# A bank for each row block of the output projection, V transposed later, V's low half behind the scaling of P

## The reference

```python
q = (x @ wq).reshape(B, S, 32, 128)      # k, v: 8 heads; rope on q and k
scores = einsum('bqhgd,bshd->bhgqs', qg, k) * 128 ** -0.5
allowed = (j <= i) & (j > i - 128)       # sliding window
attn = softmax(where(allowed, scores, min), axis=-1)
out = einsum('bhgqs,bshd->bqhgd', attn, v).reshape(B, S, 4096)
x = x + out @ wo
```

## Time and profile before

| | us |
|---|---|
| median of 3 runs (746.28 to 747.5) | 746.47 |
| the profiled execution, its own time | 746.33 |
| its span | 744.6 |
| PE busy | 717.2 |
| DVE busy | 601.0 |
| ACT busy | 413.3 |
| POOL busy | 396.5 |

### The profile page before, as it was taken

How to read it: one execution, slowest core, us unless ns; L and a number is a source line. 1 busy time by engine, 2 the same in 40 slices (tenths; PEclk the granted TensorE clock), 3 DMA queues, 4 the chain that set the end, 5 groups by cost and what they waited for, 6 DMA issues and landing times.

```text
span 744.6 us, 13949 instructions
## 1 busy us (share of the span) xinstructions
PE 717.2 (96%) x3692; PEld 603.1 (81%) x3692; DVE 601.0 (81%) x2060; ACT 413.3 (56%) x1122; POOL 396.5 (53%) x466
## 2 busy tenths in 40 slices
PE   8899789999999999999999999999999999998998
PEld 5787667888888888888888888888888888887786
DVE  6898778877887888878887888788878887788795
ACT  3324475657655676556655766576656665754320
POOL 0674268634864477438653765367535863462420
PEclk9999999999999999999999999999999999999999
DMA  8240003100220022002200120013000310030002
GB/s 266 73 158 16 0 3 98 43 1 2 73 70 1 0 70 70 0 0 70 56 14 0 56 70 14 0 32 94 15 0 0 99 28 1 1 114 1 0 31 85
DMA packets 25843, 32.13 MB, mean 43 GB/s; under 512 B 5833, under 2 KB 14281, under 8 KB 25298
## 3 DMA queue, kind: packets, MB, share of 16 engines
q1 hardware_dynamic: 25232, 30.69, 13.1%
q10 hardware_dynamic: 578, 1.05, 0.4%
HBM read 27.54 MB, written 4.19 MB: 43 GB/s over the span
## 4 chain that ended last, share of the span: by engine, by line
PE 70%; DVE 20%; issue 5%; ACT 3%; DMA 1%; POOL 1%; DVEq 0%; SPq 0%; ACTq 0%
PE bank L1102 26%; PE bank L1160 19%; PE bank L1145 6%; PE bank L1124 5%; PE bank L1068 5%; PE bank L1132 3%; DVE prob L822 2%; DVE rot L787 2%; DVE oT_lo L834 2%; DVE prob L814 1%; DVE sm L807 1%; PE bank L1121 1%; DVE rot L778 1%; ACT prob L550 1%; DVE pT_hi_lo L828 1%
## 5 line engine op out<-in xcount | busy, mean ns | idle before, releaser
L368 POOL TENSOR_TENSOR swap<-swap,rope 128x512 f32<-128x512 f32 x80 | 110.1, 1377 | 129.8 <-ACT swap L523 129.8
L550 ACT ACTIVATE prob<-sm,nmax 128x128 f32<-128x128 f32 x128 | 51.5, 403 | 151.4 <-DVE prob L814 150.4
L375 POOL TENSOR_SCALAR_AFFINE_SELECT pT_hi_lo<-pT_hi_lo 128x256 fp32r<-128x256 f32 x128 | 52.3, 409 | 140.3 <-DVE pT_hi_lo L828 139.8
L523 ACT ACTIVATE swap<-bank 64x512 f32<-64x512 f32 x160 | 94.9, 593 | 10.6 <-PE bank L1102 6.7
L558 ACT ACTIVATE pT_hi_lo<-bank 128x256 fp32r<-128x256 f32 x128 | 48.9, 382 | 71.5 <-PE bank L1132 50.6
L822 DVE TENSOR_SCALAR prob<-prob,rinv 128x128 f32<-128x128 f32 x256 | 83.3, 367 | 4.5
L385 POOL TENSOR_TENSOR q_lo<-rot,q_hi 128x512 fp32r<-128x512 f32 x64 | 82.6, 1291 | 6.9 <-ACT q_hi L531 6.9
L1160 PE MATMUL bank<-wo_hi,oT_hi 128*128 128x512 f32 x256 | 74.6, 413 | 5.0 <-DVE x L841 5.0
L828 DVE TENSOR_TENSOR pT_hi_lo<-bank,pT_hi_lo 128x256 fp32r<-128x256 f32 x128 | 53.6, 418 | 29.4 <-ACT pT_hi_lo L558 29.2
L1102 PE MATMUL bank<-xnT_hi,wq_hi 128*128 128x512 f32 x256 | 71.4, 391 | 2.2 <-DVE v_lo L798 1.4
L1102 PE MATMUL bank<-xnT_lo,wq_hi 128*128 128x512 f32 x256 | 73.4, 389 | 0.0
(11 more groups left out here) (150 smaller groups left out, 1768.9 us busy)
## 6 DMA issues: line engine op xcount, KB each, us to landing
raw<-in_L_attn_wq SPq DMA_DIRECT2D x32, 256.0 KB, 3.0
raw<-in_L_attn_wo SPq DMA_DIRECT2D x32, 256.0 KB, 2.6
x<-in_L_attn_x SPq DMA_DIRECT2D x4, 512.0 KB, 7.3
raw<-in_L_attn_wk SPq DMA_DIRECT2D x8, 256.0 KB, 2.7
raw<-in_L_attn_wv SPq DMA_DIRECT2D x8, 256.0 KB, 2.6
out<-x SPq DMA_DIRECT2D x8, 256.0 KB, 2.0
raw<-in_L_ffn_W_base ACTq DMA_DIRECT2D x4, 256.0 KB, 5.1
wb_keep_hi<-q_hi SPq DMA_DIRECT2D x1, 1024.0 KB, 4.9
```

The lines of the kernel that those rows point to most:

```text
L368: nc.gpsimd.tensor_tensor(w, w, tab, ALU.mult).then_inc(t2_done, 1)
L523: last = nc.scalar.activation(swap[a:a + half, m % 2, :], A[m % 2][b:b + half, :], ACT.Copy)
L550: last = nc.scalar.activation(prob[:, s % 2, lo:hi], src, ACT.Exp, bias=nmax[:, s % 2, i:i + 1], scale=-1.0, accum_out=rsum[:, s % 2, i:i ...
```

## The change

`out_project` of row block 1 writes bank 5 (`O[0]`, whose contents have been read by then) instead of bank 7, except for the very last one. It no longer waits for the add of row block 0. In exchange `values`, which overwrites bank 5, waits for the add of the block before, and row block 0 for the add that last read bank 7. `v_transpose` stands behind the first four matmuls of a half's first slot. On DVE `v_lo` moves behind `softmax_norm` in slot 0, and the add of row block 0 behind it in slots 3 and 7.

```diff
+        def wo_bank(beta, i, last):
+            return C if i == 0 or last else O[0]
...
-                        if s == 0 and not (last and hf == 1):
-                            v_lo(2 * g + hf, hf)
-                        if s % G == 3 and not start:
-                            x_add(beta - 1, (b - 1) % BATCH, 0)
                         if s % G == 0 and not (first and b < 2):
                             x_add(beta - 2, (b - 2) % BATCH, 1)
                         softmax_norm(u, s)
+                        if s == 0 and not (last and hf == 1):
+                            v_lo(2 * g + hf, hf)
+                        if s % G == 3 and not start:
+                            x_add(beta - 1, (b - 1) % BATCH, 0)
...
 # values
                 wait(pe, otlo_done, 2 * beta)
+                wait(pe, x_added, 2 * beta)
...
 # out_project
-                wait(pe, x_added, 2 * beta + i)
+                if i == 0:
+                    wait(pe, x_added, 2 * beta - 1)
+                elif last:
+                    pe.wait_ge(x_added, 2 * beta + 1)
...
-                        last = mm(C[:, :], oT[a][:, par, i, h, :], wo_s[c][:, h, :],
+                        end = mm(wo_bank(beta, i, last)[:, :], oT[a][:, par, i, h, :], wo_s[c][:, h, :],
...
 # group, PE
-                        if s == 0 and not start:
-                            v_transpose(j)
...
-                            project(j + 1, 1 - hf, FIRST[s], FIRST[s + 1], g + hf)
+                            mid = FIRST[s] + 4 if s == 0 and not start else FIRST[s]
+                            project(j + 1, 1 - hf, FIRST[s], mid, g + hf)
+                            if s == 0 and not start:
+                                v_transpose(j)
+                            project(j + 1, 1 - hf, mid, FIRST[s + 1], g + hf)
```

More of the change, by code:

```diff
@@ L835, in o_lo, with x_add @@
                                             oT[0][:, par, i, :, :].bitcast(F32), ALU.subtract).then_inc(otlo_done, 1)
-            def x_add(beta, b, i):
+            def x_add(beta, b, i, last=False):
                 dve.wait_ge(c_done, 2 * beta + i + 1)
                 wait(dve, x_added, 2 * beta + i)
-                nc.vector.tensor_tensor(x[:, 2 * b + i, :], C[:, :], x[:, 2 * b + i, :], ALU.add).then_inc(x_added, 1)
+                nc.vector.tensor_tensor(x[:, 2 * b + i, :], wo_bank(beta, i, last)[:, :], x[:, 2 * b + i, :], ALU.add).then_inc(x_added, 1)
             def ffn_start(s):
@@ L864, in group @@
                         split, m = (ENDS.get(c) if not (last and hf == 1) else None for c in (s - 1, s))
+                        if s % G == 0 and not (first and b < 2):
+                            x_add(beta - 2, (b - 2) % BATCH, 1)
+                        softmax_norm(u, s)
                         if s == 0 and not (last and hf == 1):
@@ L868, in group @@
                             x_add(beta - 1, (b - 1) % BATCH, 0)
-                        if s % G == 0 and not (first and b < 2):
-                            x_add(beta - 2, (b - 2) % BATCH, 1)
-                        softmax_norm(u, s)
                         if split is not None and split < 5:
@@ L981, in _ @@
             ht_lo(1, 0)
-            x_add(4 * KV - 1, BATCH - 1, 1)
+            x_add(4 * KV - 1, BATCH - 1, 1, last=True)
             norm_stats(2, 6)
@@ L1147, in values, with out_project @@
                     last.then_inc(pv_done, 1)
-            def out_project(beta, par, i, g):
+            def out_project(beta, par, i, g, last=False):
                 pe.wait_ge(conv_hi, wo_pos(g, G - 1) + 1)
                 pe.wait_ge(othi_done, 2 * beta + i + 1)
-                wait(pe, x_added, 2 * beta + i)
+                if i == 0:
+                    wait(pe, x_added, 2 * beta - 1)
+                elif last:
+                    pe.wait_ge(x_added, 2 * beta + 1)
                 for n, (a, c) in enumerate(((0, 0), (0, 1), (1, 0))):
@@ L1159, in out_project @@
                     for h in range(G):
-                        last = mm(C[:, :], oT[a][:, par, i, h, :], wo_s[c][:, h, :],
-                                  start=(h == 0 and n == 0), stop=(h == G - 1 and n == 2))
-                last.then_inc(c_done, 1)
+                        end = mm(wo_bank(beta, i, last)[:, :], oT[a][:, par, i, h, :], wo_s[c][:, h, :],
+                                 start=(h == 0 and n == 0), stop=(h == G - 1 and n == 2))
+                end.then_inc(c_done, 1)
             def group(g, first, last):
@@ L1174, in group @@
                         if not (last and hf == 1):
-                            project(j + 1, 1 - hf, FIRST[s], FIRST[s + 1], g + hf)
+                            mid = FIRST[s] + 4 if s == 0 and not start else FIRST[s]
[3 more added lines that the diff above has]
+                            project(j + 1, 1 - hf, mid, FIRST[s + 1], g + hf)
+                        elif s == 0:
+                            v_transpose(j)
                         elif s >= 4:
@@ L1261, in _ @@
             h_transpose(1, 0)
-            out_project(4 * KV - 1, 1, 1, KV - 1)
+            out_project(4 * KV - 1, 1, 1, KV - 1, last=True)
             lora_out(1, 0)
```

## The result

| | before | after |
|---|---|---|
| median of six runs each, us | 747.4 (746.28 to 748.39) | 753.04 (752.74 to 754.08) |
| ratio | 1 | 1.008, 95% interval 1.0067 to 1.0092 |
| profiled execution, us | 746.33 | 753.84 |
| its span, us | 744.6 | 752.1 |

The account below looks back on a forecast made before the run. TensorE, busy 96% of the span, was taken as the bound, so only its waits could yield time. 7 x 0.78 = 5.5, less 0.1, gave +5.4 us on 746.33: 751.7 us, own range 749.6 to 753, chance 0.60.

Parts of the forecast that it names:

- The bank: First half's last slot, groups 0 to 6: the 0.91 us wait for the add goes, at most -6.4 us; new waits cost nothing.
- The add behind the scaling in slot 7: On DVE in slot 7: the add there makes the rest, up to ACT's exponential, 0.24 us late.
- The later transposes: V's transposes four matmuls into a half's first slot: PE comes at about 356.2, not 355.28, hiding about 0.9 us of waiting.
- v_lo behind the scaling: Second half's head: POOL's wq_lo pair holds the scaling, v_lo follows, PE's second piece starts 0.78 us later, seven times.
- Rival A: At the second half's head POOL does not hold the scaling, pair 0.48 us: 742.9 us, chance 0.14.
- Rival B: The whole add stall goes, 6.4 us, and nothing takes its place: 739.8 us, chance 0.09.
- Rival C: Only the first scaling is held, both go when POOL's first wq_lo ends: 745.6 us, chance 0.09.
- The terms of one group: Per group, in groups 0 to 6: the second projection piece starts 0.78 us later; seven times, 5.5 us.
- Start and tail: Group 0's v_lo wait and the last half's 0.24 us delay: taken together as -0.1 us, bounds -0.5 and +0.5.
- Rival D: Second half, slots 3 to 5: the add pushes the rotation sum into POOL's multiplication, a second new wait: 754 us or above, chance 0.08.

Follow-up runs that it names:

- the short pair: The changed kernel with POOL's two wq_lo subtractions of slot 7 covering 8 of 512 columns: 744.25 us, ratio 0.9965.
- the kernel with the early pair: The changed kernel with POOL's two wq_lo subtractions placed first in slot 7, ahead of p_part and rope_lo: 748.47 us, ratio 1.0021.

## Why the prediction was right

**The size.** Forecast 751.7 against a profiled 746.33, so +5.4 us; measured +5.6 by the medians. That 753.04 is 1.3 us above the forecast, and 0.04 above the upper end of my own range, comes for 0.9 us from before, whose median is 747.4 over six runs and was 746.47 over the first three. That 5.4 and 5.6 lie so close is luck in part: the profiles without their starts differ by 6.4 us and runs at a like clock by 6.3 and 6.5, so the sum was about a microsecond short. The term that was too small is the one of a group, and it is taken apart below.

**The bank.** The 0.91 us stall is gone in all seven places, as said, and the new waits cost nothing: PE's list of waits has no new line for the add. That it doesn't show in the time is because it was passed on. With the bank alone it goes into the wait for `v_diff`.

**The add behind the scaling in slot 7.** Forecast 0.24 us of delay on DVE to the exponential. From the reciprocal to the exponential it is 3.81 us after (356.78 to 360.59), 3.58 before (353.55 to 357.13): 0.23. Its share of the total is 1.4 to 1.9 us, by the two pairs of kernels that differ in it alone (1.008 against 1.0061, 744.85 against 742.94). The working took it in and bounded what it does in the last half by 0.5; there it measures 0.6, since from the last half's transposes to the tail's projection the changed kernel takes 42.65 us, before 42.02, and the kernel with the add back ahead 41.93.

**The later transposes.** PE comes to them at 359.43, the difference for V ends at 359.33 (358.91 + 0.42): no wait, as forecast. The only wait for it in the list is one of 0.2 us in group 0's first half. The bank alone shows what is hidden: 0.50 us of idle time, and 0.67 us between where they could start (352.51 + 2.84) and where they do. I had about 0.9, of which 0.24 was the add.

**v_lo behind the scaling.** This was the term that decided. The pair was to take about 1.7 us, v_lo to start within 0.05 us of the end of POOL's second, PE to follow by 0.15: measured 1.70, 0.01 and 0.13. Rival A (not held), which the short pair produces on purpose, came out at 2.6 us under before where I had worked out 3.4. Rival B is out by the period, 78.48 us where it had 76.7. Rival C would have put v_lo 0.40 us behind the end of POOL's first wq_lo, at 362.49, and it starts at 363.33. The Trainium skill's page "SBUF — State Buffer", section "Who interferes with whom", which gives issue order as what decides, is borne out in the part it states (the pair of scalings, issued second, waits). It also fits the second scaling, which the prediction had called open, if an instruction that is held counts as issued. In after POOL's second starts (362.05) ahead of DVE's second scaling (362.10) and goes first, as at 343.25 and 343.29 in the earlier trace rows; in the kernel with the early pair DVE's instruction starts ahead of POOL's second (355.08 against 355.70) and goes first. The first scaling of after shows the same: it starts at 361.70, ahead of POOL's second, and is through at 362.17. The trace of before already had a case of VectorE first, which I had not looked up; there too it is POOL's next that is held:

```profile
348.66 1.80 DVE L787 TENSOR_TENSOR rot<-rot,swap 128x512 f32<-128x512 f32 x1
349.87 1.75 POOL L368 TENSOR_TENSOR swap<-swap,rope 128x512 f32<-128x512 f32 x1
```

Read with it, would have spoken against rival C more firmly.

**The terms of one group.** I had 0.78 us, the period grew by 0.90. From the projection to the second piece after takes 8.44 us (355.70 to 364.14), I had 8.53; less before's 7.75 that is 0.69. To this comes the restart of PE after the wait, 0.11 us (1.19 against 1.08), which I left out. The rows of the output projection take 1.17 us with the stall before them and without, and I had looked no further; the one wait for v_lo in the trace of before shows the cost (its row at 89.80 takes 1.19 us, the one at 360.19 takes 1.07). The last 0.1 is a slow drift of PE's starts over rows in which no wait is recorded; its cause stays open. Seven times 0.90 is 6.3, where I had 5.5.

**Start and tail.** Taken at -0.1 with bounds of 0.5 each way. Group 0 gave back about 0.5 us (PE's lateness falls from 1.03 to 0.53 between the transposes of its first and second half), the last half lost 0.6: together +0.1, with each part at or past its bound, so that -0.1 came out near by luck. 6.3 and 0.1 make 6.4 us, and with the 1.0 us by which after's profile is late from its start they account for 7.4 of the 7.5 by which the two spans differ.

**Rival D** (a wait for the rotation's cosine part in slot 5 of the second half). The meeting it rests on takes place:

```profile
377.61 1.29 POOL L372 TENSOR_TENSOR swap<-swap,rope 128x512 f32<-128x512 f32 x1 [0.46 <-ACT swap L527]
377.95 1.49 DVE L791 TENSOR_TENSOR rot<-rot,swap 128x512 f32<-128x512 f32 x1
...
387.55 0.69 DVE L782 TENSOR_TENSOR rot<-bank,rope 128x512 f32<-128x512 f32 x1 [0.54 <-ACT swap L527]
```

The sum is held, 1.49 us in place of 0.68, but by 387.55 DVE is idle again, waiting for ACT, and PE never waits for it. L782 ends at 388.24 and PE's row starts at 388.79, so 0.55 us is left of the 1.15 of before (383.54 and 384.69): with the 0.2 us for the weights 0.35, near the 0.3 worked out.

## What to carry to other kernels

Before you move an instruction of one engine, look at what the other engines run at its new time: here a short pair of VectorE operations moved from 2.58 to 0.90 us behind the start of GpSimd's long pair. It was held to that pair's end, and with it the operation behind it, on which TensorE waited. Removing a stall moves the next deadline forward, and it pays only as far as that one is met: the same bank was worth 1.0 us alone, 3.9 with the transposes moved, and 6.8 with v_hi ahead of the exponentials. Put what a waiting engine needs ahead of what may be held, not behind.

## What the runs showed of the hardware

- VectorE's two scalings of a 128x128 fp32 tile, 0.48 us as a pair, took 1.70 to 1.72 us when the first began 0.9 us into the first of two GpSimd subtractions, whose pair took 2.52 to 2.55 us with or without them. In the meetings shown here, the next instruction that had started first by the trace, though held, went first: GpSimd's by 0.05 us in after; VectorE's by 0.62 us in the kernel with the early pair and by 1.21 us in the kernel before, and in both GpSimd's was held (1.74 and 1.75 us in place of 1.3). In the ten traces together the rotation's sum began beside one GpSimd instruction and ahead of the next 77 times, and that next one took over 1.45 us each time.
- It doesn't hit every operation: v_lo, which reads one input from PSUM, took 0.69 us inside the same pair (banks and later transposes, at 356.61); the rotation's sum (both inputs in SBUF) took 1.21, 1.49 and 1.80 us in place of 0.68.
- After a wait in the middle of a projection TensorE's first row of four matmuls took 1.18 to 1.21 us in place of 1.07, and the row behind it started 1.02 us later in place of 0.91 (364.14 to 365.16 in after), so such a wait costs 0.1 us beyond its idle time. Behind P's transposes such a row takes 1.17 us anyway, and a wait adds nothing to it. One too short to be listed costs it too: in the kernel with the banks and the later transposes the row at 357.43 has no idle time before it, and 1.19 us.
